# Reordering a chunked recurrence: token difference and low half of r ahead of the decay levels, a masked product for the first level, the second mix ahead of the value product

## What is computed

```python
xx = shift_by_one_token(x) - x                     # token difference
xxx = x + xx * maa_x
a = tanh(xxx @ w1).reshape(B, T, 5, 32)
m = einsum('btfd,fdc->fbtc', a, w2)                # five mixes: w, k, v, r, g
xw, xk, xv, xr, xg = [x + xx * (maa_j + m_j) for j in 'wkvrg']
r, k, v, g = xr @ Wr.T, xk @ Wk.T, xv @ Wv.T, silu(xg @ Wg.T)
w = time_decay + tanh(xw @ wd1) @ wd2
decay = exp(-exp(w))
for t in range(T):                                 # 8 heads of 64
    kv = k[t][:, None] * v[t][None, :]
    y[t] = r[t] @ (S + u[:, None] * kv)
    S = decay[t][:, None] * S + kv
out = x + (group_norm(y) * ln_gamma + ln_beta) * g @ Wo.T
```

## Time and profile before

| | us |
|---|---|
| median of 3 runs | 1090.19 |
| lowest, highest | 1087.47, 1093.52 |
| the profiled execution | 1091.6 |
| its span (first to last instruction) | 1089.8 |
| PE busy in the span | 912.2 (84%) |
| DVE busy | 800.4 (73%) |
| ACT busy | 519.1 (48%) |
| POOL busy | 150.9 (14%) |

### The profile page before, as it was taken

How to read it: one execution, slowest core, us unless ns; L and a number is a source line. 1 busy time by engine, 2 the same in 40 slices (tenths; PEclk the granted TensorE clock), 3 DMA queues, 4 the chain that set the end, 5 groups by cost and what they waited for, 6 DMA issues and landing times.

```text
span 1089.8 us, 17163 instructions
## 1 busy us (share of the span) xinstructions
PE 912.2 (84%) x6778; PEld 743.8 (68%) x6794; DVE 800.4 (73%) x1190; ACT 519.1 (48%) x735; POOL 150.9 (14%) x210
## 2 busy tenths in 40 slices
PE   2557889898898988899787999999999765888885
PEld 1546788787887878888787778877888532444442
DVE  5857868778677787876839666889887786777763
ACT  5445163452534526244152434344544316787884
POOL 3001011020110201101010200000000111434431
PEclk9668899899899999989989999999999887999998
DMA  9210102001020110201303032331232312222120
GB/s 264 94 48 11 39 11 87 11 30 59 10 88 10 35 54 13 65 11 61 125 20 135 2 117 98 117 102 43 87 115 78 107 41 78 76 69 88 59 69 29
DMA packets 36944, 72.35 MB, mean 66 GB/s; under 512 B 6466, under 2 KB 7234, under 8 KB 35850
## 3 DMA queue, kind: packets, MB, share of 16 engines
q1 hardware_dynamic: 35754, 68.29, 18.9%
q0 software_dynamic: 1120, 3.10, 1.1%
HBM read 57.76 MB, written 12.58 MB: 65 GB/s over the span
## 4 chain that ended last, share of the span: by engine, by line
PE 46%; DVE 27%; issue 18%; ACT 4%; POOL 3%; DMA 2%; DVEq 0%; POOLq 0%; ACTq 0%
PE P L62 6%; PE S L673 6%; PE P L63 6%; PE P L64 6%; DVE rec L1674 4%; PE S L775 3%; PE S L62 3%; PE S L64 3%; PE S L63 3%; DVE R L958 2%; DVE xf L920 2%; DVE E L1668 2%; DVE K L961 2%; PE P L630 1%; PE P L687 1%
## 5 line engine op out<-in xcount | busy, mean ns | idle before, releaser
L673 PE MATMUL S<-R,K 128*128 128x128 f32 x896 | 118.9, 289 | 35.6 <-DVE K L961 35.6
L673 PEld LDWEIGHTS S<-R,K 128*128 128x128 f32 x896 | 112.8, 201 | 39.9 <-issue 38.6
L958 DVE TENSOR_TENSOR R<-R,D 128x512 f32<-128x512 f32 x96 | 66.8, 696 | 32.3 <-PE S L673 32.3
L371 POOL TENSOR_TENSOR sm<-sm,mhalf 128x16 f32<-128x16 f32 x8 | 30.6, 3826 | 319.4 <-DVE sm L1007 319.4
L2028 PE MATMUL P<-wq,xqT 128*128 128x512 bf16 x241 | 64.3, 388 | 10.6 <-ACT xqT L1976 10.3
L941 DVE COPY_PREDICATED A<-masks,S 128x1024 f32<-128x1024 int32 x40 | 70.0, 1750 | 0.0
L1668 DVE TENSOR_SCALAR E<-S,upper 128x2048 f32<-128x2048 f32 x16 | 37.6, 2350 | 39.2 <-PE S L1517 39.0
L2036 PE MATMUL S<-wq,hqT 128*128 128x512 bf16 x255 | 59.8, 390 | 4.2 <-ACT hqT L1981 4.2
L2084 DVE TENSOR_REDUCE s<-gc 128x1 f32<-128x2048 f32 x16 | 36.6, 2286 | 31.1 <-ACT gc L1988 31.1
L920 DVE TENSOR_TENSOR xf<-P,xx 128x1024 f32<-128x1024 f32 x40 | 48.8, 1221 | 10.1 <-PE P L630 9.4
L1674 DVE RECIPROCAL rec<-S 128x512 f32<-128x512 f32 x16 | 53.6, 3351 | 0.8 <-PE S L1532 0.7
(11 more groups left out here) (280 smaller groups left out, 2766.7 us busy)
## 6 DMA issues: line engine op xcount, KB each, us to landing
wch<-in_wff SPq DMA_DIRECT2D x32, 256.0 KB, 3.1
cwch<-in_wff SPq DMA_DIRECT2D x8, 1024.0 KB, 6.7
xt<-in_x SPq DMA_DIRECT2D x8, 512.0 KB, 4.0
y<-in_x SPq DMA_DIRECT2D x8, 512.0 KB, 3.7
out<-y SPq DMA_DIRECT2D x8, 512.0 KB, 3.4
cxt<-out SPq DMA_DIRECT2D x8, 512.0 KB, 4.2
ct<-in_ctx SPq DMA_DIRECT2D x8, 512.0 KB, 5.3
cxr<-out SPq DMA_DIRECT2D x8, 512.0 KB, 7.4
```

The source lines that it names most:

```text
L673: mm = pe.matmul(ps[:, b, k, :, :].rearrange("p a t -> p (a t)"), K[:, r % 2, T * g:T * g + T], right_tokens(g, i), start=True, stop=True)
L958: dve.tensor_tensor(right, right, wide(decay.unsqueeze(1).unsqueeze(3), right.shape), ALU.mult).then_inc(R_up, 1)
```

## The change

**DVE:** `lo(q, 4)` and `shift(p)` go to the front of the step, ahead of level 0. `maa_x` goes behind level 3. `lower_stack` goes behind level 5 and is four subtractions of 32 rows, written straight into `stack`, for one of 128 rows and four copies by ACT. `lower_g` goes behind `mix(p, 0)`, `y_front` behind `mix(p, 1)` and its sum. The first level's predicated copy becomes a product with the mask as float32, and its `absorb` (a memset of one column) goes.

**PE:** the bonus goes to L in place of X1, and waits for `aw_ready` and `A_wide` (whoever read and wrote L last) and no more for `mix_ready`; level 0 waits for `bonus_ready` instead. The transposes stand ahead of k chunk 0. r chunk 2 goes from behind the fifth part of the w1 product to ahead of level 4, r chunk 3 to behind level 4, and the w1 products behind these: the first ahead of level 5, the second behind it. `mix(p, 1)` goes ahead of the value product, directly behind `mix(p, 0)`, and waits for DVE's `mix(p, 0)`.

**ACT:** `hi(q, 4)` stands ahead of the copy to dg. The copy `ah` and the four copies of low halves go; `accept_wide(r, 5)` stands in the midst of the eight others.

```diff
     act.wait_ge(a_tanh, 2 * p + 1)
-    act.activation(ah[:, :], a4[:, :], ACT.Copy).then_inc(a_hi, 1)
-    for j in range(2):
-        stack_rows(j, 0, a4)
-        stack_rows(j, 2 * D_MIX, a4)
-    act.wait_ge(a_lo, p + 1)
-    for j in range(2):
-        stack_rows(j, D_MIX, al.bitcast(F32))
-    for j in range(2, 4):
-        stack_rows(j, 0, a4)
-        stack_rows(j, 2 * D_MIX, a4)
-        stack_rows(j, D_MIX, al.bitcast(F32))
+    for j in range(4):
+        stack_rows(j, 0)
+
+def stack_second(p):
+    for j in range(4):
+        stack_rows(j, 2 * D_MIX)
...
     act.wait_ge(a1_done, p + 1)
-    act.wait_ge(stacked, 12 * (p + 1))
+    act.wait_ge(stacked, 8 * (p + 1))
+    act.wait_ge(a_lo, 4 * p + 1)
     act.activation(a4[0:D_MIX, :], X1[0:D_MIX, 2 * T:4 * T], ACT.Tanh).then_inc(a_tanh, 1)
...
     f, s_, t_ = p is not None, q is not None, r is not None
+    if s_:
+        hi(q, 4)
     if t_:
...
             act.wait_ge(bonus_v, r)
-        act.activation(dg[:, :], X1[:, 0:2 * H], ACT.Copy).then_inc(bonus_ready, 1)
+        act.activation(dg[:, :], L[:, 0:2 * H], ACT.Copy).then_inc(bonus_ready, 1)
     if last_levels(q, r):
...
     if f:
-        stack_inputs(p)
+        stack_first(p)
+    if t_:
+        accept_wide(r, 5)
+    if f:
+        stack_second(p)
         stack_last(p)
...
     if t_:
-        accept_wide(r, 5)
         if last_levels(q, r):
...
             pe.wait_ge(ones_ready, 1)
-        pe.wait_ge(stacked, 12 * p + 5)
+        pe.wait_ge(stacked, 8 * p + 5)
+        pe.wait_ge(a_lo, 4 * p + 1)
     elif j == 1:
-        pe.wait_ge(stacked, 12 * (p + 1))
+        pe.wait_ge(stacked, 8 * (p + 1))
+        pe.wait_ge(a_lo, 4 * (p + 1))
     elif j == 3:
...
         pe.wait_ge(r_ready, 2 * (r + 1))
-        if r + 1 < PAIRS:
-            pe.wait_ge(aw_ready, r + 2)
-        if r > 0:
-            pe.wait_ge(A_wide, 3 * r)
+        pe.wait_ge(bonus_ready, r + 1)
     if i == 1:
...
         if r + 1 < PAIRS:
-            pe.wait_ge(mix_ready, 5 * (r + 2))
+            pe.wait_ge(aw_ready, r + 2)
+        if r > 0:
+            pe.wait_ge(A_wide, 3 * r)
         for b in range(2):
             for k in range(NC):
-                mm = pe.matmul(X1[:, H * b + 2 * k:H * b + 2 * k + 2], PY[:, k, T * b:T * b + T], usel[:, k, :],
+                mm = pe.matmul(L[:, H * b + 2 * k:H * b + 2 * k + 2], PY[:, k, T * b:T * b + T], usel[:, k, :],
                                start=True, stop=True)
         mm.then_inc(bonus_done, 1)
+    if f:
+        pe.wait_ge(xn_ready, 2 * (p + 1))
+        if p > 0:
+            pe.wait_ge(mix_ready, 5 * p)
+        for k in range(NC):
+            for b in range(2):
+                mm = turn(X1[:, (2 * k + b) * T:(2 * k + b + 1) * T], xt[:, b, P * k:P * k + P])
+        mm.then_inc(xn_turned, 1)
     if s_:
...
         channel_major("k", X0, 0)
-    if f:
-        pe.wait_ge(xn_ready, 2 * (p + 1))
-        if t_:
-            pe.wait_ge(bonus_ready, r + 1)
-        elif p > 0:
-            pe.wait_ge(mix_ready, 5 * p)
-        for k in range(NC):
-            for b in range(2):
-                mm = turn(X1[:, (2 * k + b) * T:(2 * k + b + 1) * T], xt[:, b, P * k:P * k + P])
-        mm.then_inc(xn_turned, 1)
     last = last_levels(q, r)
...
         x["q_chunk"](0, 1)
+    if s_:
+        if f:
+            pe.wait_ge(xnT_ready, p + 1)
+        pe.wait_ge(lo_ready, 4 * (q + 1))
+        if q == 0:
+            pe.wait_ge(wsplit_lo, 2)
+        channel_major("r", X1, 2)
+    if t_:
+        level(r, 4)
+    if last:
+        x["q_chunk"](0, 2)
+    if s_:
+        channel_major("r", X1, 3)
     if f:
...
     if t_:
-        level(r, 4)
+        level(r, 5)
     if last:
-        x["q_chunk"](0, 2)
+        x["q_chunk"](0, 3)
     if f:
...
         mm.then_inc(a1_done, 1)
-    if s_:
-        pe.wait_ge(lo_ready, 4 * (q + 1))
-        if q == 0:
-            pe.wait_ge(wsplit_lo, 2)
-        channel_major("r", X1, 2)
-    if t_:
-        level(r, 5)
-    if last:
-        x["q_chunk"](0, 3)
-    if s_:
-        channel_major("r", X1, 3)
     if t_:
...
         mix(p, 0, X0)
+        pe.wait_ge(mix_ready, 5 * p + 1)
+        mix(p, 1, X0)
     if t_:
...
         x["v_rows"](0, 0)
-    if f:
-        pe.wait_ge(mix_ready, 5 * p + 1)
-        mix(p, 1, X0)
     if s_:
...
     m = LEVELS[i]
+    if i == 0:
+        out = A[:, :, :, :, :].rearrange("p b k a (n two) -> p (b k a) n two", two=2)[:, :, :, 1]
+        got = level_ps(i).rearrange("p b k a n -> p (b k a) n")
+        dve.tensor_tensor(out, got, wide(masks[:, 0, :].bitcast(F32).unsqueeze(1), [P, 4 * NC, HALF]), ALU.mult).then_inc(A_part, 1)
+        return
     out = A[:, :, :, :, :].rearrange("p b k a (n two m) -> p (b k a) n two m", two=2, m=m)[:, :, :, 1, :]
...
             dve.wait_ge(y_done, r)
-        absorb(i)
+        if i > 0:
+            absorb(i)
         accept(i)
...
-    dve.wait_ge(a_hi, p + 1)
-    if p > 0:
-        dve.wait_ge(stacked, 12 * p)
-    dve.tensor_tensor(al[:, :], a4[:, :], ah[:, :].bitcast(F32), ALU.subtract).then_inc(a_lo, 1)
+    for j in range(4):
+        dve.wait_ge(stacked, 8 * p + j + 1)
+        dve.tensor_tensor(stack[D_MIX:2 * D_MIX, j, :], a4[D_MIX * j:D_MIX * j + D_MIX, :], stack[0:D_MIX, j, :].bitcast(F32),
+                          ALU.subtract).then_inc(a_lo, 1)
...
     closing, last = last_projections(p, q), last_levels(q, r)
+    if s_:
+        lo(q, 4)
+    if f:
+        shift(p)
     if t_:
...
-    if f:
-        shift(p)
     if t_:
...
         x["low_x"](0)
+    if t_:
+        level(r, 2)
+        level(r, 3)
     if f:
...
     if t_:
-        level(r, 2)
-    if s_:
-        lo(q, 4)
-    if t_:
-        level(r, 3)
         level(r, 4)
+        level(r, 5)
     if f:
...
         split_weight("k")
-    if t_:
-        level(r, 5)
-    if f:
-        lower_g(p)
     if first:
...
         mix(p, 0)
+        lower_g(p)
         xf_sum(p, 0)
...
         x["norm"](1)
-    if t_:
-        y_front(r)
     if f:
...
         xf_sum(p, 1)
+    if t_:
+        y_front(r)
     if t_:
...
     masks[start:start + m, i, j] = 1
+masks[:, 0] = masks[:, 0].astype(np.float32).view(np.int32)
 w1, w2 = np.asarray(inputs["L0_ffn_w1"]), np.asarray(inputs["L0_ffn_w2"])
```

## The result

The changed kernel takes **1062.35 us** (median of four runs, 1061.54 to 1064.22) beside 1090.43 for the kernel before on the same chip (1087.47 to 1093.52). The ratio is 0.9751, with an interval of 0.9722 to 0.978. That is 28 us saved; 1062.35 lies inside the range and 6.35 us above the predicted 1056.0. The profiled execution took 1061.54, with a span of 1059.7.

A forecast was written before the change was run, and what follows sets the result against it. No engine was full; PE came nearest, waiting mostly for DVE's chain ahead of levels and losing clock. Savings of 20.7, 5.5, 3, 0.8 and 4.5 sum to 34.5 us: 1091.6 to 1057.1, median 1056; range 1041 to 1074.

The forecast's parts named there:

- The step at full clock: Full step if the clock never falls: 57.4 us PE busy plus 5.15 of waits, 62.6 us.
- the clock: Full steps: 0.9 us each left as lost to PE's low clock, half the smaller loss before, giving 63.5 us.
- The rival with the clock: Clock falls as long as before or longer, 6.8 us low in each step: 2.5 for six steps, 1071; chance 0.13.
- the start: Up to the second bonus: 5.5 us from the bonus running inside its wait for mix 4, 4.5 from lower_g.
- the next step: Step 512.27, without token difference: the split of r and the masked product save some 3 us of its waits.
- The lock: Front of a full step: POOL's product of V holds DVE's token difference up, 1.75 us charged, bounds 0 and 1.9.
- The rival of 1041: POOL's lock doesn't bite and the clock stays up: 15 us less than forecast, 1041; chance 0.15.
- The masked product: Level 0 on DVE: product with the mask takes 1.22 us in place of 2.28, some 1.13 less start to start.
- the rival of 1065: Masked product costs what the predicated copy costs: 1.13 times 8, 1065; chance 0.09.
- Doesn't deliver: PE's waits ahead of levels come back elsewhere; only start and two last steps gain, 8 us: 1083; chance 0.11.
- slower: Bonus to value product: short waits pull the clock down, 20 us at 1.2 GHz per step, 1107; chance 0.06.
- lower_g's share: Start, pair 1: lower_g behind mix 0 no longer holds DVE's queue while waiting for ACT; 4.5 us, bounds 2 and 5.4.

## Why the prediction was right, and where it was off

**The step at full clock was right: 62.6 forecast, 62.28 measured.** Its two terms were each off and met: PE is busy for 58.04 (57.4 forecast) and waits 4.13 (5.15 forecast). The waits by place, forecast and measured: level 1, 0.8 and 0.31; level 2, 0.2 and none; level 3, 1.2 and 1.04; w1 product, 0.4 and 0.21; mix 1, 1.35 and 1.32; v, 0.5 and 0.52; V, 0.7 and 0.73. The four behind DVE's chain were followed, and too long by 1.04 together; DVE reached level 0 at 6.58 us from the step's start where I had 6.93.

**The term that was mis-sized is the clock: 0.9 us a step was assumed, 2.74 is measured.** Five steps make 9.2 us of it, and the better full clock length (0.3 each) gives 1.6 back: 13.1 saved for 20.7. The reasoning was that the longest wait falls from 2.5 to 1.35, so half of the smaller loss would stay. It took the clock as following the length of the longest wait. The runs show otherwise: 2.57 ahead of level 3 came with 3.4 us of low clock, 1.32 ahead of mix 1 with none, 6.8 or 10.2. The rival with the clock was priced by 6.8 low in each step, at 1071; 6.8 or 10.2 came in five of six steps, and the time lies between the forecast and it.

**The forecast of the whole was nearer than its parts.** The full steps saved 7.6 us less than forecast; the start, the next step and the rest gave 3.2 of it back, and for most of these 3.2 there was no reason in the prediction (see below).

**The lock was right.** POOL's product and the token difference exclude each other as the row of the last step said. The difference takes 2.78 in place of 1.2, and without it the step is 1.37 shorter, for 1.75 charged. The rival of 1041 had no lock and the clock up as well. With POOL moved out of the way the kernel took 1050.29, and 1040.25 in its one run at the clock of 0.952.

**The masked product was right:** 1.21 for 1.22, and undoing it costs 1.26 a step and 10.5 us in all, so the rival of 1065 (product dear) is out.

**"Doesn't deliver" and "slower" are out.** The waits for K went from 4.1 to 1.35 in a step and only 1.32 came back at mix 1. The rival "slower" needed ten and more microseconds of low clock in each step; no full step of the changed kernel had more than 10.2, and the mean was 6.1.

**The start was right in sum, wrong in parts.** First bonus to second was 70.43 and is 71.18, no gain where 5.5 was forecast. The first bonus is 11.9 us earlier (91.78 for 103.64), of which 5.15 is its own wait. The bonus now goes ahead of it, and PE stands for the same mix 4 one item further in its order, at the transposes:

```profile
97.09 1.94 PE L612 MATMUL P<-ident,xt 128*128 128x128 f32 x8 [3.46 <-DVE xf L917]
```

To the second bonus it is 11.1 for a forecast of 10, and that these meet is luck: of the two terms one came nowhere in its step. lower_g's share was 5.8 to the first bonus beside the changed kernel's trace, 3.0 to 3.6 beside those of three others, and 3.6 to the second (4.5 forecast).

**lower_g was mis-sized in the full steps.** Its term stood at the start only; of the parts that were put back one by one it is the largest, 14.6 us. The prediction let DVE's subtractions run beside level 6, but didn't see that lower_g waits for the last of ACT's copies with mix 0 behind it.

**The next step** (5.3 for 3): before it had 10.2 us of low clock, now 3.4, which is up to 3.4 of the 5.3. **The rest** (0.6 for 0.8) says little: this stretch is between 511.8 and 516.2 us long in the traces of the experiments.

**What stays open** is what else decides whether the clock falls behind the wait at mix 1. With that wait there (1.32, and 2.04 in the run with lower_g back), it fell in 5, 5, 4, 3, 2 and 2 of 6 steps in six kernels, and not at all there in the one with 2.57 ahead of level 3. The traces hold a part of the answer, which no experiment was made for. These are the six waits at mix 1 of the changed kernel:

| PE at work again | clock falls at | after | low for |
|---|---|---|---|
| 129.97 | 132.54 | 2.57 | 6.8 |
| 195.22 | 197.40 | 2.18 | 6.8 |
| 260.52 | 262.25 | 1.73 | 6.8 |
| 325.83 | 327.10 | 1.27 | 10.2 |
| 392.67 | no fall | | |
| 455.02 | 456.81 | 1.79 | 6.8 |

The first four waits are 65.3 us apart, the falls 64.85. So the falls don't keep step with the kernel; they keep a beat of their own, and each wait meets it a little later than the last one did. In the run with the levels' order back the falls are 64.85 apart too (177.95, 242.80, 307.66, 372.51, 437.36), though they stand at level 3; its steps are 64.8 long, so every step meets the beat alike, and every step has the same fall and none at mix 1. In each of the twelve traces all changes of the clock lie on one such beat. Six kernels have the wait of 1.32 at mix 1, 36 waits in all. The 16 with a fall behind them begin in one part of the beat (from 0.86 of it through its mark to 0.26), the 20 without one in the other (from 0.31 to 0.85), and the low stretch is 10.2 us long where the fall comes within 1.33 us of PE's return and 6.8 where it comes later. So whether this wait brings a fall goes with when it begins, and the number of falls hangs on how the length of a step runs against the beat. That leaves a rival to the reading by place: the 2.57 ahead of level 3 and the 1.95 ahead of v met the beat at other points than the 1.32 did. A run that only moves the start of the recurrence by a microsecond or two could tell them apart; there is none.

## What to carry to other kernels

- Where waits of 1 to 3 us keep PE from its high clock, compare kernels by the length of a step at the high clock, and count the falls apart. A fall cost 1.5 to 4.7 us, and the same wait of 1.32 brought one in 16 of 36 steps, so a difference of one or two falls between two kernels can be chance. Filling the wait with PE's own later work paid 9 us though no idle time was won.
- Before work is moved into a gap of DVE's, look at what POOL does there. If it needs the shared ports, let POOL wait until DVE reads PSUM: one wait was worth 12 us here, 6.9 of them by shorter full steps.
- An instruction that waits is priced with all that is queued behind it on its engine, in each step and not only where its wait is longest.

## What the runs showed of the hardware that I had not expected

- POOL and DVE both pay for the lock. POOL asked 0.12 us into a DVE instruction and ended 2.87 us later (1.90 alone). DVE's next instruction, issued 1.17 us into that, took 2.78 (1.23 alone). POOL got through between two DVE instructions that stood back to back: it ended at 366.05 and the long one 1.08 us later, about the time that it takes alone.
- A predicated copy of 1024 elements a partition out of PSUM takes 2.47 us at blocks of 1 and 2.46 at blocks of 2, and 1.26 at blocks of 4. The product with the mask takes 1.21 at a stride of 2.
- The clock's low stretches in the full steps are 3.4, 6.8 or 10.2 us long. Behind waits of 1.3 and 1.4 us they begin 0.9 to 2.6 us after PE is at work again (328.42 and 329.35 with mix 1 back; 129.97 and 132.54 in the changed kernel), behind the 2.57 already at its end (307.9 and 307.7). Their starts keep a beat of their own, 64.85 us apart where the steps are 65.3.
- The same kernel's runs differ by up to 12 us with the granted clock of the whole span (1065.2 at 0.942, 1053.3 at 0.956).
